# Router logits from extra columns of the v and out products in an adaLN block with linear attention and mixture of experts

## The reference

```
h   = layernorm(x) * (1 + ca) + sa
q,k,v = h Wq' + bq, h Wk' + bk, h Wv' + bv           16 heads of 8
phi(u) = (exp(u orf' / 8**0.25 - |u|^2 / (2 sqrt 8)) + 1e-6) / sqrt 32
attn  = phi(q) (phi(k)' v) / (phi(q) sum phi(k))      per head
x     = x + ga * (attn Wo' + bo)
h   = layernorm(x) * (1 + cb) + sb
e     = argmax(h gate_W + gate_b)                      8 experts, one per token
x     = x + gb * (gelu(h W1[e] + b1[e]) W2[e] + b2[e])
```

## Time and profile before

| what | us |
|---|---|
| three runs | 364.67, 361.58, 364.75 |
| median | 364.67 |
| span of the profiled execution, first to last instruction | 360.6 |
| from that span to the median | 4.07 |

### The profile page before, as it was taken

How to read it: one execution, slowest core, us unless ns; L and a number is a source line. 1 busy time by engine, 2 the same in 40 slices (tenths; PEclk the granted TensorE clock), 3 DMA queues, 4 the chain that set the end, 5 groups by cost and what they waited for, 6 DMA issues and landing times.

```text
span 360.6 us, 13729 instructions
## 1 busy us (share of the span) xinstructions
PE 338.8 (94%) x4823; PEld 263.9 (73%) x4823; DVE 271.2 (75%) x1104; ACT 265.1 (74%) x644; POOL 213.2 (59%) x262
## 2 busy tenths in 40 slices
PE   6899999899988999998999999999999999999994
PEld 5445765566465566646665669999989999999993
DVE  3456997898879789878887978887677676666653
ACT  2688988799878888977888756676656667666761
POOL 3142386776667757857854618846767455545554
PEclk9999999999999999999999999999999999999999
DMA  7174656774566547444432467445657665545410
GB/s 233 50 253 166 210 184 221 259 243 160 177 227 205 176 167 230 163 132 156 153 133 100 149 163 227 142 118 150 194 161 269 209 184 147 147 128 135 137 38 12
DMA packets 40211, 60.47 MB, mean 168 GB/s; under 512 B 5426, under 2 KB 28086, under 8 KB 40016
## 3 DMA queue, kind: packets, MB, share of 16 engines
q1 hardware_dynamic: 33776, 42.54, 39.9%
q0 software_dynamic: 6368, 17.05, 12.5%
HBM read 28.63 MB, written 19.34 MB: 133 GB/s over the span
## 4 chain that ended last, share of the span: by engine, by line
PE 60%; ACT 15%; DMA 10%; DVE 6%; issue 5%; POOL 1%; SPq 1%; DVEq 1%; POOLq 0%; ACTq 0%
PE ps_proj L1350 16%; PE ps_feat L1337 9%; DMA qmix<-qsqs 9%; PE ps_proj L1132 6%; PE ps_den_gate L1337 4%; PE ps_proj L1182 4%; PE ps_kv L1337 4%; ACT qf L627 3%; ACT qvals L606 2%; ACT shared L588 2%; PE ps_kv L1198 2%; PE ps_out L1330 2%; ACT den L656 2%; ACT shared L581 2%; ACT kvm L600 2%
## 5 line engine op out<-in xcount | busy, mean ns | idle before, releaser
L545 POOL DMA_INDIRECT out<-kf,modb x71 | 70.1, 987 | 52.4 <-DVE kf L1060 47.0
L507 POOL DMA_INDIRECT experts_lists<-pay,slot x64 | 65.9, 1030 | 43.4 <-DVE slot L893 29.5
L1350 PE MATMUL ps_proj<-w2sb,qf 128*128 x568 | 75.0, 275 | 0.4 <-ACT qf L690 0.4
L1350 PEld LDWEIGHTS ps_proj<-w2sb,qf 128*128 128x128 f32 x568 | 68.9, 192 | 0.6 <-issue 0.6
L681 ACT ACTIVATE xT<-ps_out 128x128 f32<-128x128 f32 x71 | 19.7, 277 | 44.8 <-PE ps_out L1330 44.1
L1055 DVE TENSOR_TENSOR kf<-ps_proj,firsts_sb 128x128 f32<-128x128 f32 x71 | 20.7, 291 | 34.6 <-PE ps_proj L1350 22.6
L690 ACT ACTIVATE qf<-ps_feat,shared 128x128 f32<-128x128 f32 x144 | 40.9, 374 | 0.0
L1337 PE MATMUL ps_feat<-xT,shared 128*128 128x128 f32 x288 | 38.8, 277 | 1.5 <-issue 0.9
L1337 PEld LDWEIGHTS ps_feat<-xT,shared 128*128 128x128 f32 x288 | 35.0, 192 | 2.8 <-issue 1.7
L1132 PE MATMUL ps_proj<-shared,wsb 128*128 128x512 f32 x62 | 33.3, 620 | 1.0 <-ACT shared L581 0.4
L977 DVE COPY shared<-firsts_sb 128x516 f32 x71 | 31.4, 442 | 1.6 <-issue 1.5
(11 more groups left out here) (189 smaller groups left out, 890.3 us busy)
## 6 DMA issues: line engine op xcount, KB each, us to landing
modb<-experts_lists SPq DMA_DIRECT2D x71, 196.0 KB, 2.8
xall<-in_x SPq DMA_DIRECT2D x16, 256.0 KB, 3.0
pay<-modb SPq DMA_DIRECT2D x16, 256.0 KB, 3.0
qmix<-qvals SPq DMA_DIRECT2D x30, 128.0 KB
qmix<-qsqs SPq DMA_DIRECT2D x30, 128.0 KB
modb<-modulation_rows SPq DMA_DIRECT2D x4, 768.0 KB, 5.2
firsts_sb<-in_firsts SPq DMA_DIRECT2D x8, 322.0 KB, 4.2
w2sb<-in_w SPq DMA_DIRECT2D x8, 256.0 KB
```

The costliest lines, as they stand in the source:

```text
L507: g_.indirect_dma_start(out=lists, in_=pay[b.home][:, t, :], in_offset=None, out_offset=bass.IndirectOffsetOnAxis(ap=slot[b.home][:, t:t + ...
L545: g_.indirect_dma_start(out=rows_out, in_=yb[u], in_offset=None, out_offset=bass.IndirectOffsetOnAxis(ap=token, axis=0), bounds_check=last ...
L1350: ins = mm(Y[u % 2][:, 0:D], g[u % R4][:, c * P:(c + 1) * P], w2sb[:, bass.ds(e * DFF + c * D, D)], start=(c == 0), stop=(c == FC - 1))
```

## The change

**Router logits.** The gate's product over h2 is taken apart by linearity. The centred gate weights, scaled by (1 + cb), become 8 more columns beside Wv * (1 + ca), so `v_project` writes 136 columns instead of 128 per tile, and 8 more beside Wo * ga, so `out_project` does too. The logits are then, per token, std1 * (v columns) + a constant of the batch - (out columns), times rstd2, plus another constant. This removes the transposes of h2, the gate's product and transpose, and ScalarE's copies L631 and L635. It adds on DVE, per batch, `gate_x_part`, `gate_constant`, `gate_sum`, and four instructions in place of one in `experts`.

**Modulation.** (1 + ca) is multiplied into the projection weights of each batch on DVE (`scaled_weights`, 128x384, and `gate_weights`, a copy of 8 columns); sa becomes a bias per batch; ScalarE's `modulate` is now a plain copy. bo * ga comes as a fifth modulation row (`BOG`). wo is kept per batch, so nothing waits before writing it.

**Routing one batch behind.** experts, slots, rank and scatter in batch b are of batch b-1 (POOL's scatter b-2); `KNOWN` is 14; only batch 15 is left for the second phase, finished at k = 19 instead of 31.

**Orders.** PE projects q before k, and `rank` comes after `attend`, in front of the next `k_features`. ScalarE takes the q values and squares before the k values. On DVE the statistics and `normalise1` no longer come before `residual`; `scale_h2` is woven into the argmax. x is a ring of 8 batches (`xring`), statistics are taken 4 batches ahead.

```diff
-KNOWN = B - 3
+KNOWN = B - 2
+XR = 8
+VT = D + E
-ROWS = 4
+ROWS = 5
...
@@ POOL
+                g_.tensor_tensor(std1[:, par, lo:hi], ve1[:, lo:hi], rstd1[:, par, lo:hi], ALU.mult)\
+                    .then_inc(s_std1, 1)
...
             def batch(b, first=False, second=False, last=False, ahead=True):
-                if not first:
+                if not first and not second:
+                    scatter(b + -2)
+                if first:
+                    rstd1_of(3)
+                else:
                     rstd2_of(b + -1, rows_of=None if second else b + -2)
-                if ahead and b.par == 0:
-                    rstd1_of(b.half + 3, b=b + 2)
-                if not first and not second:
-                    scatter(b + -2, (0, 1))
+                if b.par == 1 and b.v + 3 < B:
+                    rstd1_of(b.half + 4)
                 gated(b, first)
...
@@ ScalarE
                 q_pair(b, 1, first)
+                if not last:
+                    q_values(b + 1)
                 kvm_copy(b)
                 if not last:
+                    q_squares(b + 1)
                     k_values(b + 1)
                     k_squares(b + 1)
-                    q_values(b + 1)
...
@@ DVE
+            def scaled_weights(b):
+                if b.v >= 2:
+                    dve.wait_ge(s_proj, 3 * b.v - 3)
+                v.tensor_scalar(wp[b.par][:, 0:3 * P], wsb[:, 0:3 * P], ca1[:, b.v:b.v + 1], None, ALU.mult)
+            def gate_weights(b):
+                v.tensor_copy(wp[b.par][:, 3 * P:3 * P + E], gcc[:, b.v, :]).then_inc(s_wg, 1)
...
+            def experts_and_h2(b, between=None):
+                for t in range(LT):
+                    ins = v.scalar_tensor_tensor(out=lg[:, t, :], in0=lg[:, t, :], scalar=rstd2[:, t:t + 1],
+                                                 in1=gate_sb[:, b.v, :], op0=ALU.mult, op1=ALU.add)
+                s.mark(ins)
+                scale_h2(b, 0)
                 s.wait()
                 s.mark(v.tensor_reduce(out=top[:], in_=lg[:], op=ALU.max, axis=AX.X))
+                scale_h2(b, 1)
...
             def batch(b, first=False, second=False, last=False, ahead=True):
...
                 if not first:
                     residual(b + -1)
+                    gate_sum(b + -1)
+                gate_x_part(b)
+                if ahead:
+                    scaled_weights(b + 2)
+                    gate_weights(b + 2)
+                if first:
+                    dve.wait_ge(s_gtab, 1)
+                gate_constant(b)
+                if not first:
                     second_stats(b + -1)
...
+                if not first and b.v + 4 < B:
+                    stats = x_stats(b + 4, b.par)
+                    if b.par:
+                        first_moments((b + 3).half + 1, marked=stats)
+                kv_values(b, first)
+                if last:
+                    block_columns(0)
...
+                if not first:
+                    centre_h2(b + -1)
+                if last:
+                    table_rows(0)
+                if first:
+                    eps_values(b)
+                else:
+                    experts_and_h2(b + -1, between=b)
+                if ahead:
+                    normalise1(b + 2, lo=LT // 2)
...
+                elif not first:
+                    slots(b + -1)
...
                 attention(b)
...
@@ PE
             def batch(b, first=False, second=False, last=False, ahead=True):
                 k_features(b, first)
-                if not first and not second:
-                    transpose_h2(b + -2, first=third)
-                v_project(b, last)
+                v_project(b, first, last)
                 if not first:
                     out_project(b + -1)
-                if not first and not second:
-                    gate(b + -2)
                 q_features(b, first)
-                if not first and not second:
-                    gate_transpose(b + -2)
+                if first:
+                    gate_constants()
                 if not last:
                     transpose_xn(b + 1)
                 kv_product(b, first)
                 if not last:
-                    project(b + 1, 0)
-                if not first and not second and not last:
-                    rank(b + -2, first=third)
+                    project(b + 1, 1)
                 kv_transpose(b, first)
                 if not last:
-                    project(b + 1, 1)
+                    project(b + 1, 0)
                 attend(b)
+                if last:
+                    pe.wait_ge(s_blk, 1)
+                if not first:
+                    rank(b + -1, counted=0 if b.v == KNOWN else None)
```

585 lines of the change are left out of this document (305 added, 280 removed).

## The result

The kernel after takes 386.39 us (median of four runs, 385.83 to 386.43), the one before beside it 363.46. The ratio is 1.064 [1.059, 1.069]: slower, and 15.7 us above the forecast of 370.7, outside its range. The profiled span is 384.0 us, 23.4 above the 360.6 of before.

What follows compares the result with a forecast made beforehand. PE bounds the kernel before, at 94% of the span; after the change DVE's period of 13.0 us would. Terms 2.7 + 2.8 + 2.8 - 2.3 = +6.0 on 360.6: span 366.6, median 370.7 us, range 358 to 382.

Steps and rivals of the forecast that it cites:

- the sum: DVE's instructions and its wait for the out product added up: a period of 13.0 us, 178.4 us for 14 periods.
- the lock: Rival: POOL's addition to x holds up DVE once in each of 14 batches, 0.65 us each, 379.8 us; chance 0.20.
- B: The 14 periods from first to last residual: DVE's longer period makes them 178.4 us against 175.65, +2.8 us.
- A: Start to first residual: later modulation products and more DVE work put it at 32.3 instead of 29.58 us, +2.7.
- C: Last residual to the fourth block's product: later block table, argmax and weight copies make it 15.6 against 12.8 us, +2.8.
- D: Between the blocks, after the fourth block's product starts: PE loses work and the count's wait goes, -2.3 us.
- POOL may be the one that waits: Argument against the lock: POOL, not DVE, may be held up when they meet, and nothing waits for POOL there.
- The step from the span to the median: The 4.07 us by which the earlier median exceeded its profiled span, carried over: span 366.6, median 370.7.
- DVE has room: Rival: new small instructions fall into DVE's old 2.15 us of idling, period 12.0, 359.0 us in all; chance 0.22.
- the disappearance of the shuffle's wait: In the batches, the wait for the shuffled q squares, 7.7 us in 9 batches before, would be gone.

Runs made afterwards that it cites:

- e5_xb_early_again: Changed kernel with POOL's scaling of wo and addition to x moved ahead of the scatter, from batch 2 on; 370.68 us, ratio 1.026 to the kernel before.
- e4_weights_on_act: Changed kernel with the scaling of the projection weights moved from DVE to ScalarE for batches 2 to 15, on a slower chip; 413.32 us, ratio 1.066.
- f1_xb_stats: `e5_xb_early_again` with the statistics of batch b+4 moved ahead of the residual on DVE, on a slower chip; 406.54 us, ratio 1.064.
- f2_xb_stats_centre: `f1_xb_stats` with h2's centring ahead of kvT on DVE and the scatter's last tile behind POOL's deviation, slower chip; 384.24 us, ratio 1.005.

## Why the prediction was wrong

**The mechanism of the sum was right: DVE's queue and its wait for the out product set the period.** DVE idles 1.29 us before each residual (taken at 1.30), and the gate's small instructions and the weights came within hundredths. The logits, the scaling and the argmax together take 2.23 us where 2.5 was taken. With the lock taken away but for batch 1, the 14 periods are 178.0 us; the sum said 178.4. The kernel then takes 370.68 us; the forecast was 370.7. Both agreements are luck in part. Within B, the ten periods of batches 2 to 11 are 12.62 on average instead of 13.0, 3.7 less in all; the last three are 2.2 more than forecast, and that of batch 1 is 14.84 instead of 13.8, with the meeting that is left in it. In the total, the span of `e5_xb_early_again` is 368.4 where the sum gives 366.6: A is 2.4 more than forecast, C 0.4, B 0.4 less and D 0.6.

**The step that failed is the lock.** The prediction had it in sight, in its own paragraph, and left it out of the sum. It was made a rival at 0.20, with 0.65 us for one meeting in each batch, 379.8 in all. It decides 12.6 us in B (190.57 less 178.0) and 0.9 in C, 13.5 in all; the medians say 13.45, but in these C's clock gives 1.0 more and A takes 0.4. Batch 1 pays another 1.2, an estimate from its rows, in both kernels. Three things were wrong. First, its chance: the paragraph on the lock itself put POOL's addition beside centring, logits and scaling, and "POOL may be the one that waits" had no row; the earlier trace rows showed that DVE was the one. Second, its size: the earlier trace rows shows one DVE instruction that begins 0.54 us into POOL's 1.34, so 0.65 is the rest of one addition. A full meeting costs DVE what POOL's two instructions last (1.75 us, from 136.91 to 138.66) less what DVE gets done meanwhile (0.5): 1.23 us (2.36 less 1.13). The prediction gave the rule of the Trainium skill, "SBUF — State Buffer", section "Who interferes with whom", and said that by it the loss could be the whole of wo and the addition; it put no number to this. 14 x 1.2 = 16.8 would have given 387.5, near the 386.4 measured, but that nearness would have been luck too: in B the runs give the lock 12.6 in 13 batches, since in the last three another wait takes half of it, and A and C add what the lock does not.

Third, the prediction named only centring, logits and scaling, and didn't ask where POOL stands in odd batches, in which it makes one more pair of powers. There it meets oh (0.39 instead of 0.19) and `normalise1` (1.60 instead of 0.60), a tensor_scalar with one tensor operand in SBUF. The same section of the Trainium skill, "Who interferes with whom" on the page "SBUF — State Buffer", says that a tensor_scalar can enter a mode that uses both port pairs, in which it contends with GpSimd, and that whoever issues first has the shared pair for the whole instruction while the other is fully blocked. The rows agree with the second: of the two instructions of `normalise1` in the row at 126.73 the first begins 0.01 us after POOL's addition and takes 1.35 us, to 0.08 after the addition's end, the second 0.33. That `normalise1` is in such a mode no run here shows, only that it is held up.

**The step from the span to the median was wrong by 1.7 us.** The prediction carried 4.07 over from before. In the kernel after the median is 2.39 above the span, in `e5_xb_early_again` 2.28, and in the profiled executions of the runs the time of an execution is 1.75 to 1.94 above its own span. So most of the 4.07 was no time around the instructions: the profiled execution of before was itself some 2 us faster than the median. It hides 1.7 us of the miss, which is 17.4 in the span (384.0 against 366.6) and 15.7 in the median.

**Term A (+2.7, measured +6.0).** kvT of batch 0 came at 27.33 instead of 24.6. With TensorE's clock at 1.00 and the weights off DVE (`e4_weights_on_act`) kvT comes at 24.18 and the first residual at 32.57, and the forecasts were 24.6 and 32.3; with 0.33 for the weights the new work of DVE and PE was short by about 0.6. What was missed is that TensorE fell to 1.2 GHz between 8 and 14 us, worth about 3 us, which it did in neither profile of the kernel before. Why it falls in one execution or order of the setup and not in another stays open; PE had idled 0.91 us before the first modulation products in both kernels.

**Term B** apart from the lock: late batches were priced at 1.12 us less each for the missing statistics. Without the lock they are 0.35 less (12.27 against 12.62). There DVE waits 0.5 to 0.8 us at kvT for the key-value product and 0.3 for POOL's deviation, so PE's way through out product, features and key-value product seems to hold the period at 12.2; no run tests that on this chip. PE's work in a batch is 11.6 us (23.22 for two), where the prediction had 11.3. The forecast had PE's way shorter by 0.4 than DVE's, and that can be right only while DVE has the statistics.

**Term C (+2.8, measured +5.2):** of the 2.4 more, 0.9 are a meeting with POOL and 0.8 to 1.0 the clock after PE's idling.

**Term D (-2.3, measured -2.9)** and the disappearance of the shuffle's wait were right.

**"DVE has room" (0.22)** was wrong, as the mean period of 12.62 in batches 2 to 11 shows also without the lock (it needed one under 12.3). What the change took from PE and ScalarE was worth nothing, because the path had moved to DVE.

## What to carry to other kernels

When an instruction of GpSimd moves, look up on the timeline what VectorE does at its new place, in every kind of batch, and price the meeting by the whole length of the GpSimd instructions, less what VectorE gets done meanwhile; if it lies on the path, it belongs in the sum and not among the rivals. Where one engine waits for a round trip (here 1.29 us), that is the place for the other's blocking instruction: moving one call gave back 13.5 us. On the first chip the lock-free kernel is still 2.6% slower than the one before, and the best version was level with it on the slower chips; none beat it.

## What the runs showed that I had not expected

- Three of four chips ran the same program 5% slower (the kernel before, 382.67 against 363.77 us), and not evenly: the batches by 1%, the blocks by 10%. Of two orders of the same work one (`f1_xb_stats`) took 22 us more than the other (`f2_xb_stats_centre`) there, with gaps of 0.4 to 1.1 us inside one group of 64 small products. A gain found on one chip can be missing on the next.
- TensorE's granted clock fell to 0.50 for 3 to 7 us at the start in 15 of 18 profiled executions of changed orders with much the same work, and moved the first residual by about 3 us. Two executions of one kernel can differ in it, so a single profile doesn't show what an edit does to the clock at the start.
